# Attention's preparation folded into the attention stage: four token tiles in front, twelve in the loop

## The chip, the cores and the metric

The kernel runs on one core of a Trainium2 chip. A core has a matrix engine (TensorE, PE in the rows; PEld are its weight loads), a vector engine (VectorE, DVE), a scalar engine (ScalarE, ACT), a general engine (GpSimd, POOL) and a queue engine that issues transfers (SyncE, SP). PSUM is the memory that PE writes its results to, SBUF the working memory, DRAM the memory outside. The metric is the device time of one execution in microseconds (us); lower is better.

## What is computed

Four batches of 512 tokens with 512 features pass two layers. The part that matters here is the attention of the second layer:

```python
x = x + _L0_xattn_ref(ctx_512, _layernorm(x), ...)      # graph attention
x = x + _L0_ffn_ref(_layernorm(x), ...)                 # 32 experts, top 4
x = x + _L1_xattn_ref(_layernorm(x), ctx_512, ctx_512)  # this stage
x = x + _L1_ffn_ref(_layernorm(x), ...)                 # 32 experts, top 8

def _L1_xattn_ref(q, k, v):          # q [4, 512, 512], k = v = ctx_512 [4, 512, 128]
    D = 512 // 32; G = 32 // 8       # 16 per head, 4 query heads per key head
    qh = q.reshape(B, S, 8, 4, 16).transpose(0, 2, 3, 1, 4)
    kh = k.reshape(B, S, 8, 16).transpose(0, 2, 1, 3)
    scores = einsum('bkgsd,bktd->bkgst', qh, kh) / sqrt(16)
    out = einsum('bkgst,bktd->bkgsd', softmax(scores), vh)
```

## The kernel before

Five stages run one after the other, each with its own semaphores and a barrier of all engines at its end: `graph_attention`, `open_ffn`, `attention_prepare` (L1576), `attention` (L1758), `capped_ffn`. The change touches the third and the fourth.

**Preparation.** Queries and keys are handed to attention as sums of three bf16 parts (`PARTS`), so that bf16 products of parts give an fp32 result. A unit is one 128x512 tile to be turned: 4 units of keys (one for each batch, four 128x128 pieces of `ctx_sb`) and 16 of tokens. For a token unit DVE computes statistics (L1721 to L1726), ACT the square root (L1683), DVE the scale and shift (L1731, L1732), and ACT or DVE in turn the normalised tile `xn` (L1692, L1739). PE transposes the four pieces into one of four PSUM banks (L1676). ACT rounds to the first part (L1699), DVE takes the difference `left` (L1754), ACT rounds that to the second part (L1703), POOL subtracts again for the third (L1644). SP stores each part to the DRAM tensors `q_parts` and `k_parts`, three transfers for a unit (L1656, L1659). Four places (`PLACES`) of parts are used in turn; a place is written again when its stores have landed (`stored`).

**Attention.** There are 32 groups: 4 batches by 8 key heads, with 4 query heads each. For a group the contraction rows of `kT` and `qT` hold seven products of parts, named by `K_PART` and `Q_PART` (7 x 16 = 112 rows, `PAIR_ROWS`), and 3 rows for the negated row maxima (115, `ROWS_ALL`). In front of the loop SP loads the keys of batch 0 and the queries of groups 1 to 3, ACT the queries of group 0, then the context and, once batch 0's keys have landed, the keys of the other batches (L2038 to L2047). The row maxima of groups 0 and 1 are computed ahead (`LEAD` = 2): per group eight pairs of matmuls (`maximum`, L1938) into two PSUM tiles, each pair reduced by DVE (L2074). POOL splits the maxima into parts (`split_maxima`, L2135 to L2140), PE transposes them (L1968), ACT copies them to `mrows` (L2029), and SP moves them into `qT` by three DMAs (`put_maxima`, L1873) and waits until they have landed.

The loop has one body for each group, with the work of three groups in it. PE issues 16 score matmuls of the group G (L1948), each freed for reuse by ACT's exponential (L2023); the 8 pairs of maxima of G + 2; the weighting of values with the exponentials (`weigh`, L1959), in four steps; the transposes of the maxima of G + 1 and of the output of G - 1 (L1976). Scores, maxima and output take turns in three PSUM banks (`SR` = 3), in an order that `use` writes down at build time (`uses`, `frees`). ACT runs the 16 exponentials, and copies the maxima and the output (L2035). DVE reduces the maxima and divides the output (L2079, L2083), POOL splits maxima, takes the values of the next group (L2148) and adds the old tokens (L2158). SP's body waits until all scores of G are done, loads the queries of G + 4 by seven transfers (L1867), puts the maxima of G + 2, waits for the new tokens (`x_ready`), stores them (L1907) and loads old tokens (L1884):

```python
                def body(G, k, ahead):
                    if not known(G) or G + QR < GROUPS:
                        sp.wait_ge(s_ps, G * SCORES + SCORES)
                        load_q(G + QR, k)
                    if ahead:
                        put_maxima(G + LEAD, (k + LEAD) % QR)
                    sp.wait_ge(x_ready, G + 1)
```

The semaphore waits and the program order on each engine are all that sets the order of the work.

## Time and profile before

| | |
|---|---|
| median of 3 runs | 2141.94 us (2138.0 to 2146.16) |
| the profiled execution | 2139.37 us |
| its span in the trace | 2137.6 us |
| mean granted TensorE clock | 0.909 of full speed |
| busy: PE, DVE, ACT, POOL | 84%, 66%, 50%, 41% |
| preparation, first to next stage's first instruction | 1149.65 to 1211.66 us |
| attention's first instruction to first score matmul | 1211.66 to 1254.88 us |
| attention's loop and end | 1254.88 to 1650.98 us, the next stage's first transfer |

A row of the timeline gives start and duration in us, engine, line of the kernel, operation, output and inputs, a count, and in brackets how long the engine was idle before and what ended that. "SPq" and "ACTq" are transfers issued by SP and ACT; their duration is that of issuing, not of moving the data. In a view of windows PEclk is the granted TensorE clock as a share of full speed, and DMA share the mean busy share of the 16 DMA engines.

### The profile page before, as it was taken

What the parts mean: (1) busy time and instruction counts of PE and PEld (TensorE: products, weight loads), DVE (VectorE), ACT (ScalarE), POOL (GpSimd) and SP (SyncE); (2) the same over time, 40 slices, a digit from 0 to 9 for tenths busy, and PEclk for the clock granted to TensorE, in tenths of its full rate; (3) what the DMA queues carried; (4) which work ended last, traced back from release to release, by engine and by line L of the source; (5) the groups of instructions that cost most, each with busy time, mean ns of one, the idle gap of its engine ahead of it and who ended that gap; (6) DMA issues with size and microseconds to landing.
All of it is one profiled execution on the core that took longest, in us unless ns stands there. A gap on an engine that the chain in (4) does not pass through costs nothing. (4 is left out here: it accounts for less than half of the span.)

```text
span 2137.6 us, 32682 instructions
## 1 busy us (share of the span) xinstructions
PE 1795.9 (84%) x9679; PEld 1025.0 (48%) x9679; DVE 1406.1 (66%) x2807; ACT 1062.3 (50%) x2149; POOL 881.9 (41%) x949
## 2 busy tenths in 40 slices
PE   4689877998548999999993279999997539999997
PEld 2344443444334555555551123333332538888885
DVE  5887877788684666566553478888883765545543
ACT  5588877878332333333332347777776412222222
POOL 5476676668103545555542311111111014444442
PEclk8699988999768999999996579999999759999998
DMA  5111211111455889889655752222221718999993
GB/s 148 55 40 40 83 62 55 40 46 35 147 152 126 177 189 236 224 196 230 122 103 157 158 103 62 57 69 56 62 64 44 267 42 221 230 235 234 230 236 58
DMA packets 202146, 272.01 MB, mean 127 GB/s; under 512 B 83484, under 2 KB 121852, under 8 KB 200956
## 3 DMA queue, kind: packets, MB, share of 16 engines
q1 hardware_dynamic: 156315, 166.52, 25.9%
q0 software_dynamic: 38544, 97.02, 22.5%
q10 hardware_dynamic: 7121, 6.44, 1.6%
q8 instruction: 82, 1.34, 0.3%
q14 instruction: 84, 0.69, 0.1%
HBM read 200.25 MB, written 69.17 MB: 126 GB/s over the span
## 5 line engine op out<-in xcount | busy, mean ns | idle before, releaser
L2074 DVE TENSOR_REDUCE a_negmax<-a_m 128x2 f32<-128x1024 f32 x256 | 304.2, 1221 | 97.2 <-PE a_m L1938 97.2
L291 POOL TENSOR_TENSOR g_near<-g_mask,g_tb 128x512 f32<-128x512 f32 x256 | 322.5, 1282 | 100.0 <-DVE g_emin L545 99.1
L2023 ACT ACTIVATE a_prob<-a_s 128x512 f32<-128x512 f32 x512 | 274.3, 595 | 83.4 <-PE a_s L1948 83.3
L1464 PE MATMUL f_gu_bank<-f_wgu,f_xT 128*128 x768 | 265.5, 489 | 2.9 <-ACT f_xT L1512 2.9
L1258 PEld LDWEIGHTS s_gu_bank<-s_xT,s_wgu 128*128 128x128 f32 x2048 | 240.8, 193 | 31.8 <-issue 27.5
L374 PE MATMUL g_pt<-g_ident,g_p 128*128 128x128 f32 x1024 | 173.5, 299 | 87.1 <-DVE g_pT L554 82.1
L1258 PE MATMUL s_gu_bank<-s_xT,s_wgu 128*128 128x128 f32 x2048 | 241.4, 277 | 1.6 <-ACT s_xT L1288 1.6
L1426 POOL DMA_INDIRECT out<-f_y,f_ids x96 | 151.2, 1575 | 209.5 <-DMA out<-f_y,f_ids 167.6
L475 ACT ACTIVATE g_p<-g_e,g_emin 128x512 f32<-128x512 f32 x256 | 183.4, 716 | 96.0 <-DVE g_emin L545 95.2
L374 PEld LDWEIGHTS g_pt<-g_ident,g_p 128*128 128x128 f32 x1024 | 122.3, 150 | 217.5 <-DVE g_pT L554 142.5
L1464 PEld LDWEIGHTS f_gu_bank<-f_wgu,f_xT 128*128 128x128 f32 x768 | 146.3, 191 | 125.8 <-issue 48.6
L554 DVE COPY g_pT<-g_pt 128x512 f32<-128x512 f32 x256 | 175.3, 685 | 44.5 <-PE g_pt L374 43.1
L545 DVE CUSTOM_DVE_ANT_0 g_e<-g_near,g_h 128x512 f32<-128x512 f32 x256 | 173.0, 676 | 39.9 <-issue 27.0
L1948 PE MATMUL a_s<-a_qT,a_kT 115*128 115x512 bf16 x512 | 179.8, 385 | 8.0 <-DMA a_qT<-a_mrows 6.6
L1938 PE MATMUL a_m<-a_kT,a_qT 112*128 112x512 bf16 x512 | 160.2, 396 | 27.3 <-DMA a_kT<-a_one_rows 25.1
L1234 POOL DMA_INDIRECT out<-s_y,s_ids x64 | 101.7, 1588 | 192.8 <-ACT s_y L1294 167.3
L1481 PE MATMUL f_y_bank<-f_wd,f_actT 96*128 x384 | 180.5, 593 | 0.0
L460 ACT ACTIVATE g_h<-g_tb,g_s 128x512 f32<-128x512 f32 x256 | 172.8, 675 | 0.0
L1542 DVE COPY f_actT<-f_at_bank 96x256 f32<-96x256 f32 x96 | 40.4, 421 | 171.8 <-PE f_at_bank L1473 170.2
L1404 POOL DMA_INDIRECT f_row<-f_x_rows,f_ids x96 | 102.2, 1064 | 106.4 <-issue 103.7
L1319 DVE TENSOR_SCALAR s_den<-s_en 128x256 f32<-128x256 f32 x64 | 20.1, 315 | 184.3 <-ACT s_en L1301 111.9
L404 PE MATMUL g_o<-g_pT,g_feat 128*64 128x512 f32 x512 | 137.8, 640 | 0.9 <-DVE g_res L578 0.9
(291 smaller groups left out, 2767.2 us busy)
## 6 DMA issues: line engine op xcount, KB each, us to landing
s_wgu<-in_L_ffn_w_gate_up SPq DMA_DIRECT2D x32, 1024.0 KB
f_wgu<-in_L_ffn_gate_up_proj SPq DMA_DIRECT2D x32, 768.0 KB
s_wd<-in_L_ffn_w_down SPq DMA_DIRECT2D x32, 512.0 KB
a_qT<-q_parts SPq DMA_DIRECT2D x217, 64.0 KB, 2.4
g_tb<-neighbours SPq DMA_DIRECT2D x8, 1536.0 KB, 8.0
f_wd<-in_L_ffn_down_proj SPq DMA_DIRECT2D x32, 384.0 KB
q_parts<-p_part SPq DMA_DIRECT2D x48, 128.0 KB, 2.3
g_tb<-neighbours SPq DMA_DIRECT2D x8, 512.0 KB, 4.3
```

The lines of the kernel that those rows point to most:

```text
L291: pool.tensor_tensor(near[:, n % LAG, :], mask[slot][:, local % NT, :], t_all[k % SLOTS][:, local // NT, :], ALU.add).then_inc(near_ready, 1)
L374: last = nc.tensor.transpose(pt_bank[n % PT_BANKS][:, c, :], prob[:, n % PROBS, c * P:(c + 1) * P], ident[:, :])
L460: nc.scalar.activation(h_bank[n % H_BANKS][:, :], t_all[k % SLOTS][:, h, :], ACT.Relu, scale=4.0, bias=s_high[k % SLOTS][:, t, h:h + 1]).t ...
L475: nc.scalar.activation(prob[:, n % PROBS, :], eneg[:, n % LAG, :], ACT.Exp, scale=-1.0, bias=emin[:, n % LAG:n % LAG + 1], accum_out=rsum[ ...
L545: V.tensor_tensor_reduce(out=eneg[:, n % LAG, :], in0=near[:, n % LAG, :], in1=h_bank[n % H_BANKS][:, :], scale=-1.0, scalar=3.0e38, op0=A ...
L554: V.tensor_copy(probT[:, n // PAIR % RING, hh, :, t * P:(t + 1) * P], pt_bank[n % PT_BANKS][:, :, :]).then_inc(pt_ready, 1)
L1258: last = nc.tensor.matmul(gu_bank[j % TR][:, f, :], wgu[:, e % RE, c, f * P:(f + 1) * P], xT[j % TR][:, c, :], start=(c == 0), stop=(c == ...
L1464: last = nc.tensor.matmul(gu_bank[j % TR][:, 0:F], xT[j % TR][:, c, :], wgu_flat[:, bass.ds(place_of[j] + c * F, F)], start=(c == 0), stop ...
L1481: last = nc.tensor.matmul(y_bank[j % TR][:, :], actT[j % TR][:, c, :], wd_flat[:, bass.ds(place_of[j] + c * D, D)], start=(c == 0), stop=( ...
L1948: nc.tensor.matmul(bank_of("score", G, n)[:, :], group_keys(G, ROWS_ALL, slice(tt * P, (tt + 1) * P)), qT[k][0:ROWS_ALL, head, :], start=T ...
L2023: nc.scalar.activation(prob[n][:, :], bank_of("score", G, n)[:, :], ACT.Exp).then_inc(p_ready, 1)
L2074: V.tensor_reduce(negmax[k % RING][:, 2 * half:2 * half + 2, head], m_bank[i % RING][:, :, :], X_AXIS, ALU.max, negate=True).then_inc(m_re ...
```

## The change

`attention_prepare` goes. Its work becomes part of `attention`:

- In front of the loop eight units are done: keys of batch 0, the four token tiles of batch 0, then keys of batches 1 to 3. They use the PSUM tiles of the maxima (`m_bank`). The parts of a unit lie in one tile, and one transfer stores all three.
- The other twelve token tiles are done in the loop, one for each of groups 0 to 3 and 8 to 15 (`late_at`): PE transposes it between two score matmuls into a bank of the ring of three, ACT copies it out (`copy_unit`), and POOL makes all three parts and the difference (`all_parts`). Tiles 4 to 7 are normalised by ACT in front of the loop, tiles 8 to 15 by POOL, each in the body of the group ahead. Their statistics are DVE's, in groups 2 to 5, and the square root is ACT's, in the middle of group 6.
- SP loads the keys of batches 1 to 3 in the loop, two transfers in each of four groups; the values of a batch are copied in groups 0 to 2.
- `q_parts` has another layout: the features within a chunk of 128 are ordered by depth, then by head, and the orders of `K_PART` and `Q_PART` are changed, so that the queries of a group come by three transfers in place of seven, of 48, 48 and 16 rows.
- SP stores a unit's parts behind the transfers of its body; the first key units and the loads of `kT` and `qT` are issued in a new order.

The diff, cut ("..." marks what is left out; the removed stage is left out whole, `root`, `first_part`, `second_part`, `statistics`, `variances`, `scales`, `difference`, `third_part` and `copy_values` do what their likes in the removed stage did):

```diff
-K_PART = (0, 0, 0, 1, 1, 2, 1)
-Q_PART = (0, 1, 2, 0, 1, 0, 2)
+K_PART = (0, 0, 0, 1, 1, 1, 2)
+Q_PART = (0, 1, 2, 0, 1, 2, 0)
...
-    TURN_AT, OUT_AT = 9, 7
+    DC = D // P
+    TURN_AT, OUT_AT, UNIT_AT = 9, 7, 4
+    PLACES = 4
+    units = [("keys", 0)] + [("tokens", t) for t in range(NT)] + [("keys", b) for b in range(1, B)]
+    FIRST = len(units)
+    units += [("tokens", t) for t in range(NT, TT)]
+    late_group = list(range(NT)) + list(range(KV, KV + 2 * NT))
+    late_at = {G: i for i, G in enumerate(late_group)}
+    Q_RUNS = ((0, PARTS), (PARTS, PARTS), (2 * PARTS, 1))
+    FINAL_STATS = 6
...
+                if n == UNIT_AT and G in late_at:
+                    use(("unit", late_at[G]), turned_ready, late_at[G] + 1)
...
+        def by_head(row):
+            return row.rearrange("p (c x d) -> p c x d", c=DC, d=HD)
+
+        def by_depth(row):
+            return row.rearrange("p (c d x) -> p c x d", c=DC, d=HD)
...
-                    flat = q_parts.rearrange("j b f s -> j (b f) s")
-                    for r, j in enumerate(Q_PART):
-                        sp.dma_start(qT[k][r * HD:(r + 1) * HD, :, :],
-                                     flat[j, bass.ds(G * GD, GD), :].rearrange("(h d) s -> d h s", d=HD)).then_inc(q_in[k], 16)
+                    b, g = divmod(G, KV)
+                    if g == 0 and b > 0:
+                        for r in range(PLACES):
+                            sp.wait_ge(stored[r], 16 * (2 + b))
+                    heads = q_parts[b, g // 2, :, :, :].rearrange("j (d x) s -> (j d) x s", x=2 * GQ)[:, g % 2 * GQ:(g % 2 + 1) * GQ, :]
+                    for r, count in Q_RUNS:
+                        sp.dma_start(qT[k][r * HD:(r + count) * HD, :, :], heads[0:count * HD, :, :]).then_inc(q_in[k], 16)
...
+                def load_keys(b, r):
+                    if r == 0:
+                        sp.wait_ge(stored[b], 16 * 2 if b else 16)
+                    if r < len(K_PART):
+                        sp.dma_start(kT[r * HD:(r + 1) * HD, b * KV:(b + 1) * KV, :],
+                                     k_parts[b, K_PART[r], :, :].rearrange("(h d) t -> d h t", h=KV)).then_inc(k_in[b], 16)
...
+                def store(u):
+                    what, i = units[u]
+                    for j in range(PARTS):
+                        sp.wait_ge(part_ready[j], u + 1)
+                    if what == "keys":
+                        target = k_parts[i, :, :, :].rearrange("j p (c s) -> p c j s", c=DC)
+                    else:
+                        target = q_parts[i // NT, :, :, :, i % NT * P:(i % NT + 1) * P].rearrange("c j p s -> p c j s")
+                    sp.dma_start(target, part[:, u % PLACES, :, :, :]).then_inc(stored[u % PLACES], 16)
+
+                def load_tokens(first, count, s):
+                    sp.dma_start(tok[:, first:first + count, :],
+                                 tokens[first * P:(first + count) * P, :].rearrange("(t p) d -> p t d", p=P)).then_inc(tok_in[s], 16)
...
+                load_tokens(0, NT // 2, 0)
+                load_tokens(NT, NT, 2)
                 sp.wait_ge(consts, 4)
-                sp.dma_start(kT[PAIR_ROWS:ROWS_ALL, 0:KV, :], bass.AP(one_rows, 0, [[N, PARTS], [0, KV], [1, N]])).then_inc(k_in[0], 16)
+                load_keys(0, len(K_PART))
+                for u in range(3):
+                    store(u)
+                for r in range(len(K_PART)):
+                    load_keys(0, r)
+                for u in range(3, 5):
+                    store(u)
+                for t in range(NT):
+                    sp.wait_ge(stored[(1 + t) % PLACES], 16 * ((1 + t) // PLACES + 1))
+                load_q(0, 0)
                 load_q(1, 1)
-                sp.wait_ge(k_in[0], 16 * (len(K_PART) + 1))
+                for u in range(5, FIRST):
+                    store(u)
...
+                    if G < 2:
+                        load_tokens((2 + G) * NT, NT, 3 + G)
+                    b, step = G // KV + 1, G % KV - 1
+                    if b < B and 0 <= step < 4:
+                        load_keys(b, 2 * step)
+                        load_keys(b, 2 * step + 1)
+                    if G in late_at:
+                        store(FIRST + late_at[G])
...
+                def late_unit(i):
+                    if i < NT:
+                        pe.wait_ge(xn_act, NT // 2 + i + 1)
+                    else:
+                        pe.wait_ge(xn_pool, i - NT + 1)
+                    bank_free("unit", i)
+                    turn(FIRST + i, bank_of("unit", i))
...
+                    if i == 0 and G % KV == 0:
+                        pe.wait_ge(k_in[G // KV], 16 * (len(K_PART) + 1))
                     if i == 0:
-                        pe.wait_ge(q_in[k], 16 * len(Q_PART) * (G // QR + 1))
+                        pe.wait_ge(q_in[k], 16 * len(Q_RUNS) * (G // QR + 1))
...
+                for u in range(FIRST):
+                    first_unit(u)
+                pe.wait_ge(left_ready, FIRST)
                 for G in range(LEAD):
                     for i in range(PAIRS):
                         maximum(G, G, i)
...
+                        if n + 4 == UNIT_AT and G in late_at:
+                            late_unit(late_at[G])
                         if d < NT - 1:
...
+                act.dma_start(ctx_sb[:, 0:NT, :], ctx_dram[0, :, :].rearrange("(t p) f -> p t f", p=P)).then_inc(ctx_in[0], 16)
+                act.dma_start(tok[:, NT // 2:NT, :], tokens[NT // 2 * P:N, :].rearrange("(t p) d -> p t d", p=P)).then_inc(tok_in[1], 16)
+                act.dma_start(ctx_sb[:, NT:TT, :], ctx_dram[1:B, :, :].rearrange("b (t p) f -> p (b t) f", p=P)).then_inc(ctx_in[1], 16)
+                first_part(0)
+                second_part(0)
+                root(0, NT, 0)
+                norm(0)
+                norm(2)
+                first_part(1)
+                for u in range(2, FIRST):
+                    first_part(u)
+                    second_part(u - 1)
+                second_part(FIRST - 1)
+                root(NT, NT, 1)
+                for t in range(NT, 2 * NT):
+                    norm(t)
...
+                        if n + 1 == UNIT_AT and G in late_at:
+                            copy_unit(late_at[G])
+                        if n + 1 == 2 * GQ and G == FINAL_STATS:
+                            root(2 * NT, 2 * NT, 2)
...
+                statistics(range(NT // 2))
+                difference(0)
+                statistics(range(NT // 2, NT))
+                variances(0, NT)
+                scales(0, NT, 0)
+                norm(1)
+                norm(3)
+                for u in range(1, FIRST):
+                    difference(u)
+                copy_values(0)
+                statistics(range(NT, 2 * NT))
+                variances(NT, NT)
                 for G in range(LEAD):
                     for i in range(PAIRS):
                         maximum(G, G, i)
...
+                        if G == 0 and i == 2:
+                            scales(NT, NT, 1)
...
+                    if G + 1 < B:
+                        copy_values(G + 1)
+                    if FINAL_STATS - 4 <= G < FINAL_STATS:
+                        t = 2 * NT + 2 * (G - FINAL_STATS + 4)
+                        statistics(range(t, t + 2))
+                    if G == FINAL_STATS - 1:
+                        variances(2 * NT, 2 * NT)
+                    if G == FINAL_STATS:
+                        scales(2 * NT, 2 * NT, 2)
...
+                def all_parts(i):
+                    u = FIRST + i
+                    source = turned[i % RING][:, :].rearrange("p (c s) -> p c s", c=DC)
+                    pool.wait_ge(turned_ready, i + 1)
+                    pool.wait_ge(stored[u % PLACES], 16 * (u // PLACES))
+                    pool.tensor_copy(part_of(u, 0), source).then_inc(part_ready[0], 1)
+                    pool.wait_ge(part_ready[0], u + 1)
+                    pool.tensor_tensor(left_of(u), source, part_of(u, 0), ALU.subtract).then_inc(left_ready, 1)
+                    pool.wait_ge(left_ready, u + 1)
+                    pool.tensor_copy(part_of(u, 1), left_of(u)).then_inc(part_ready[1], 1)
+                    pool.wait_ge(part_ready[1], u + 1)
+                    pool.tensor_tensor(part_of(u, 2), left_of(u), part_of(u, 1), ALU.subtract).then_inc(part_ready[2], 1)
...
+                def norm(t):
+                    pool.wait_ge(scale_ready, 3)
+                    pool.wait_ge(unit_ps, FIRST + t - 2 * NT + 1)
+                    pool.tensor_scalar(by_depth(xn[:, t % NT, :]), by_head(tok[:, t, :]), rstd[:, t:t + 1], nbias[:, t:t + 1], ALU.mult, ALU.add).then_inc(xn_pool, 1)
+
                 def take_values(G, k):
+                    if G % KV == 0:
+                        pool.wait_ge(val_all_ready, G // KV + 1)
...
+                for u in range(FIRST):
+                    third_part(u)
                 split_maxima(0, 0)
-                pool.wait_ge(val_all_ready, 1)
-                pool.sem_inc(turns, 1)
                 take_values(0, 0)
 
                 def body(G, k, ahead):
                     if not (known(G) and G == GROUPS - 1):
                         split_maxima(G + 1, (k + 1) % QR)
                         take_values(G + 1, (k + 1) % QR)
+                    if G in late_at:
+                        all_parts(late_at[G])
                     if not (known(G) and G == 0):
                         add_tokens(G - 1, (k - 1) % QR)
+                    if G + 1 in late_at and late_at[G + 1] >= NT:
+                        norm(late_at[G + 1] + NT)
...
-    q_parts = nc.dram_tensor("q_parts", (PARTS, B, D, N), BF16).ap()
-    k_parts = nc.dram_tensor("k_parts", (PARTS, B, ctx_512.shape[2], N), BF16).ap()
+    q_parts = nc.dram_tensor("q_parts", (B, D // P, PARTS, P, N), BF16).ap()
+    k_parts = nc.dram_tensor("k_parts", (B, PARTS, P, N), BF16).ap()
...
-    attention_prepare(nc, tokens, ctx_512, q_parts, k_parts)
```

Three places in the order of instructions. PE, body of group 2 of the loop; L1948/L1892 are scores, L1938/L1882 maxima, L1959/L1903 `weigh`, L1976/L1920 the output's transposes. Before:

```order
L1959 MATMUL a_o<-a_prob,a_val 32x512 x4
L1948 MATMUL a_s<-a_qT,a_kT 128x512 x2
L1938 MATMUL a_m<-a_kT,a_qT 128x512 x2
L1948 MATMUL a_s<-a_qT,a_kT 128x512
L1938 MATMUL a_m<-a_kT,a_qT 128x512 x2
L1976 MATMUL a_s<-a_ident,a_oT 128x128 x4
```

and now:

```order
L1903 MATMUL a_o<-a_prob,a_val 32x512 x4
L1851 MATMUL a_s<-a_ident,a_xn 128x128 x4
L1892 MATMUL a_s<-a_qT,a_kT 128x512 x2
L1882 MATMUL a_m<-a_kT,a_qT 128x512 x2
L1892 MATMUL a_s<-a_qT,a_kT 128x512
L1882 MATMUL a_m<-a_kT,a_qT 128x512 x2
L1920 MATMUL a_s<-a_ident,a_oT 128x128 x4
```

The four transposes of a token tile stand between the weighting and the next scores.

ACT, groups 6 and 7; L2023/L1969 are exponentials, L2029/L1975 the copy of maxima, L2035/L1981 the copy of the output. Before:

```order
L2035 ACTIVATE a_oT<-a_o 128x512
L2023 ACTIVATE a_prob<-a_s 128x512 x5
L2029 ACTIVATE a_mrows<-a_s 12x512
L2023 ACTIVATE a_prob<-a_s 128x512 x11
L2035 ACTIVATE a_oT<-a_o 128x512
```

and now:

```order
L1981 ACTIVATE a_oT<-a_o 128x512
L1969 ACTIVATE a_prob<-a_s 128x512 x4
L1985 ACT_TABLE_LOAD
L1985 ACTIVATE a_std<-a_std 128x8
L1969 ACT_TABLE_LOAD
L1969 ACTIVATE a_prob<-a_s 128x512
L1975 ACTIVATE a_mrows<-a_s 12x512
L1969 ACTIVATE a_prob<-a_s 128x512 x11
L1981 ACTIVATE a_oT<-a_o 128x512
```

The square root stands in the middle of the exponentials, with a table load on either side.

SP, from the start of the preparation to the first `put_maxima` (L1873/L1770). Before:

```order
L1648 DMA p_ctx<-in_ctx 128x16x128
L1650 DMA p_tok<-out 128x4x512 x4
L1656 DMA k_parts<-p_part 128x512 x12
L1659 DMA q_parts<-p_part 128x4x128 x48
L1629 UNCONDITIONAL_BRANCH
L1862 UNCONDITIONAL_BRANCH
L1887 DMA a_kT<-k_parts 16x8x512 x7
L1889 DMA a_kT<-a_one_rows 3x8x512
L1867 DMA a_qT<-q_parts 16x4x512 x21
L1884 DMA a_x_old<-out 128x4x64 x2
L1873 DMA a_qT<-a_mrows 1x4x512 x6
```

and now:

```order
L1764 DMA a_tok<-out 128x2x512
L1764 DMA a_tok<-out 128x4x512
L1750 DMA a_kT<-a_one_rows 3x8x512
L1761 DMA k_parts<-a_part 512x3x128
L1761 DMA q_parts<-a_part 128x12x128 x2
L1747 DMA a_kT<-k_parts 16x8x512 x7
L1761 DMA q_parts<-a_part 128x12x128 x2
L1741 DMA a_qT<-q_parts 48x2048 x2
L1741 DMA a_qT<-q_parts 16x2048
L1741 DMA a_qT<-q_parts 48x2048 x2
L1741 DMA a_qT<-q_parts 16x2048
L1761 DMA k_parts<-a_part 512x3x128 x3
```

Of 60 stores in front of the first loads of keys and queries three stand there now, and five in front of the first queries.

## Rows read from the trace of the kernel before

**Rows 1.** Windows view of core 0, one row for each stretch; columns in its first row.

```profile
core 0: us, PE busy (x) PEld busy (x) DVE busy (x) ACT busy (x) POOL busy (x), PEclk, DMA share, GB/s
1149.65:1171.65 22.00, 6.67 (x28) 5.56 (x28) 9.52 (x20) 8.55 (x14) 5.26 (x6) 0.58 0.88 298
1171.65:1211.65 40.00, 13.29 (x52) 9.72 (x52) 25.36 (x53) 21.21 (x39) 19.13 (x16) 0.54 0.67 165
1211.65:1225.65 14.00, 0.00 (x0) 0.00 (x0) 0.00 (x0) 0.02 (x1) 1.53 (x7) 0.50 1.07 127
1225.65:1254.85 29.20, 16.99 (x36) 2.97 (x36) 20.18 (x20) 1.87 (x2) 2.76 (x14) 0.50 1.03 177
1254.85:1645.85 391.00, 387.68 (x2268) 132.54 (x2268) 301.31 (x302) 301.84 (x575) 64.83 (x241) 0.99 0.21 56
```

**Rows 2.** Timeline, start of preparation: start, duration, engine, line, operation.

```profile
1149.71 0.90 SPq L1648 DMA_DIRECT2D p_ctx<-in_ctx  x1
...
1159.05 2.47 DVE L1721 BATCH_NORM_STATS2 p_stats<-p_tok 128x6 f32<-128x512 f32 x4 [28.73 <-DMA p_tok<-out]
...
1163.41 1.28 ACT L1683 ACT_TABLE_LOAD   x1
...
1164.70 0.20 ACT L1683 ACTIVATE p_std<-p_std 128x4 f32<-128x4 f32 x1
```

**Rows 3.** Timeline, start of attention.

```profile
1211.66 3.89 SPq L1887 DMA_DIRECT2D a_kT<-k_parts  x7
...
1225.68 1.86 PE L1938 MATMUL a_m<-a_kT,a_qT 112*128 112x512 bf16 x4 [25.06 <-DMA a_kT<-a_one_rows]
...
1226.73 9.42 DVE L2074 TENSOR_REDUCE a_negmax<-a_m 128x2 f32<-128x1024 f32 x8 [22.41 <-PE a_m L1938]
```

**Rows 4.** Groups by line from 1140 to 1256 us: count, busy us, mean ns, idle before.

```profile
L1644 POOL TENSOR_TENSOR p_part<-p_left,p_part 128x512 bf16<-128x512 f32 x20 | 23.9, 1205 | 32.3 <-ACT p_part L1703 31.9 <-DVE p_left L1754 0.4
...
L1703 ACT ACTIVATE p_part<-p_left 128x512 bf16<-128x512 f32 x20 | 12.5, 625 | 8.1 <-DVE p_left L1754 8.1
...
L1699 ACT ACTIVATE p_part<-p_bank 128x512 bf16<-128x512 f32 x20 | 11.8, 588 | 29.0 <-PE p_bank L1676 23.9 <-DMA q_parts<-p_part 4.9 <-DMA k_parts<-p_part 0.2
```

**Rows 5.** Timeline, end of the start of attention.

```profile
1237.31 7.00 ACTq L2047 DMA_DIRECT2D a_kT<-k_parts  x7
...
1240.16 9.42 DVE L2074 TENSOR_REDUCE a_negmax<-a_m 128x2 f32<-128x1024 f32 x8 [4.00 <-PE a_m L1938]
...
1244.96 19.84 SPq L1873 DMA_DIRECT2D a_qT<-a_mrows  x6
...
1254.88 1.04 PE L1948 MATMUL a_s<-a_qT,a_kT 115*128 115x512 bf16 x2 [6.57 <-DMA a_qT<-a_mrows]
```

**Rows 6.** Timeline of ACT, one group of the loop.

```profile
1399.67 2.12 ACT L2023 ACTIVATE a_prob<-a_s 128x512 f32<-128x512 f32 x4 [0.72 <-PE a_s L1948]
1402.51 2.12 ACT L2023 ACTIVATE a_prob<-a_s 128x512 f32<-128x512 f32 x4 [0.72 <-PE a_s L1948]
1405.05 0.60 ACT L2035 ACTIVATE a_oT<-a_o 128x512 f32<-128x512 f32 x1 [0.43 <-PE a_o L1959]
...
1417.28 0.60 ACT L2035 ACTIVATE a_oT<-a_o 128x512 f32<-128x512 f32 x1 [0.43 <-PE a_o L1959]
```

**Rows 7.** Timeline of SP's DMA issues in the same group.

```profile
1409.71 1.82 SPq L1873 DMA_DIRECT2D a_qT<-a_mrows  x3
1412.72 0.40 SPq L1907 DMA_DIRECT2D out<-a_x_new  x1
...
1413.72 3.34 SPq L1867 DMA_DIRECT2D a_qT<-q_parts  x7
```

**Rows 8.** Timeline of DVE and POOL in the same group.

```profile
1412.55 2.36 DVE L2074 TENSOR_REDUCE a_negmax<-a_m 128x2 f32<-128x1024 f32 x2 [0.48 <-PE a_m L1938]
...
1415.10 0.20 POOL L2135 CAST a_mbf<-a_negmax 128x16 bf16<-128x16 f32 x1 [6.22 <-DVE a_negmax L2074]
```

**Rows 9.** DMA view, 1400 to 1500 us: median us from issue to landing.

```profile
a_qT<-q_parts SPq DMA_DIRECT2D x58, 64.0 KB, 2.3
```

289 lines of the change are left out of this document (114 added, 175 removed).

## The prediction

> **What bounds the kernel now.** I first cut the span into stretches with the windows view [rows 1]. The first three, 76.0 us, are the preparation, its barrier and the loads of keys and queries; in the third no engine but POOL works. The fourth, 29.2 us, is the row maxima of the first two groups. The fifth, 391 us, is the loop, where PE is busy at a granted clock of 0.99 (2.4 GHz) and POOL for 65 us. So the change can win in the first four (105 us, before the first score) and lose in the fifth. The page's chain of waits is of no use here, since it reaches back only into the last stage.
>
> Next I read who waits in those stretches. The preparation starts on transfers: DVE's statistics come 9.4 us after its start (1159.05), behind 2 MB in one queue [rows 2]. From there a unit costs ACT 588 + 625 ns and POOL 1205 ns, 20 times [rows 4]; 40 us for its second part is more than 1.2 us a unit. Attention's first matmul then waits 25 us, the last 14 of them for keys and queries (1211.66 to 1225.68) [rows 3]. The loop is a cycle between PE and ACT: four exponentials, 0.72 us of waiting for the next score, 2.84 us in all; a group is 12.23 us (1405.05 to 1417.28) [rows 6]. DVE waits 0.48 us in each round of two reductions, POOL 6.2 us at a stretch [rows 8].
>
> **The work in front of the loop.** I measure from 1149.65 to the first reduction of maxima, 1226.73 [rows 3]: 77.1 us. In the new order (all are estimates from the rows named):
> - Loads. Two queues issue smaller first pieces: 0.25 MB of context, then tokens in pairs. With 2 MB landed in 9.4 us [rows 2], I put the first statistics at 6.5 us and the second pair at 8.
> - Scales. Before, statistics start at 1159.05 and the root runs at the end of the table load, 1164.69, 5.6 us later [rows 2]. The table load now lies beside the second pair; I take root at 10.3, first normalised tile at 11.6, its transposes at 12.9.
> - Units 1 to 4 at 1.25 us each (ACT, POOL [rows 4]): the third part of unit 1 is ready at 16.3, of unit 2 at 17.5, of unit 4 at 20.
> - SP stands in the way once: behind the store of unit 2 come seven loads of keys, 3.9 us of issue [rows 3], so unit 3 is stored at 22. The keys are 0.9 MB; the third stretch moved 127 GB/s, with the transfer engines fully busy [rows 1], so they take 7 us, and the stores of units 3 and 4 queue behind them: landed at 28.5.
> - Queries of group 0: 1.6 us of issue for three transfers (0.48 each before [rows 7]) and 2.3 us to land [rows 9]: 32.5. A matmul pair and its wait add 1.05 (1225.68 to 1226.73 [rows 3]): **33.5 us**. DVE has finished the last difference, the values and four statistics at about 32.5, so it doesn't come later.
>
> Gain 77.1 - 33.5 = **43.6 us**. Bounds: 29 if the keys come at twice that rate and units never wait for a place; 40 if each store lands only behind all of the 3 MB of loads.
>
> **From the first reduction to the first score** it took 28.2 us (1226.73 to 1254.88): two times 9.4 us of reductions, 4.0 us of splitting and transposing between them, and in the end a wait of 6.6 for the maxima's rows [rows 3, 5]. ACT couldn't copy the maxima before 1244.3, since it issued 21 key loads until then (ACTq, 7.0 us the last seven), and the rows issued at 1244.96 took 9.9 us among them to be used [rows 5]. The key loads are now SP's, in the loop. What is left is 9.4 + 4 + 9.4 = 22.8: gain **5.3 us** (3 to 6).
>
> The barrier goes with the stage; its 2 to 5 us are within the 77.1. Instructions of the preparation don't vanish, twelve units of 20 move.
>
> **Twelve units in the loop.** Each adds four transposes to PE and a copy to ACT, in front of the same score. The output has the same pair, and so have the maxima: 12.23 - 4 x 2.84 = 0.87 us for both [rows 6], so 0.43 us each, since the 0.60 us copy runs beside transposes. At this place ACT already has the output's copy behind its 0.43 us wait [rows 6], so a second copy there can't hide in that wait; PE's four transposes run beside the first. I take 0.55. The ceiling is both in a row, 0.60 + 0.57 = 1.17. 12 x 0.55 = **6.6 us** (5.2 to 14).
>
> POOL gets four operations of at most 1.2 us and, for the last eight, a normalisation: 6.2 us against 6.2 of idle time at a stretch and 2.5 more ahead of it [rows 4, 8]. The new tokens come up to 3.5 us later, while SP is still waiting for its maxima's rows until 1412.72 [rows 7]. Cost nothing; if that cover is gone, the store of x slips, which nobody waits for in under a group.
>
> **Square root in group 6.** ACT does load, root, load: 1.28 + 0.20 + 1.28 = 2.76 us [rows 2], of which the round's wait of 0.72 [rows 6] hides one: **2.0 us** (2.0 to 2.8). In the row the root follows the load at once (1163.41 + 1.28, then 1164.70), nothing more is paid. The Trainium skill (ScalarE: Activation LUTs, What ACT_TABLE_LOAD costs) counts a drain of about 1.38 us for each switch as well; by that page it would be an estimated 4.8, and the rest of this text stands without it.
>
> **DVE's extra work** in groups 0 to 5: statistics of a pair 1.23 us (2.47 / 2 [rows 2]) in groups 2 to 5, a copy of values of about 0.4 in groups 0 to 2, and the variances of eight tiles, about 1 us, in group 5. It comes between two groups, where 0.48 us of wait [rows 8] and the slack of the second PSUM tile (I put it at 0.7: PE is let go by the reduction before the last) take it up: nothing for 0.4, 0.1 for 1.23, 0.5 for 1.6 (group 2), 1.1 for 2.2 (group 5): **1.8 us**. Floor 0, ceiling all of it, 7.5.
>
> **SP in the loop.** Seven query transfers of 3.34 us of issue [rows 7] become three, 1.6; two key loads (1.0) and a store (0.5) come in. Issue hardly changes, and is off the path. What is queued behind is `put_maxima`, which is the next rival's matter.
>
> **Sum.** 43.6 + 5.3 - 6.6 - 2.0 - 1.8 = 38.5 us. Against the profiled execution, 2139.37 - 38.5 = 2100.9; the median of the runs was 2.6 above that execution, so **2103 us**.
>
> **Rivals.**
> - *The terms of the loop are near their ceilings* and the front at 36: gain 41.1 + 3, less 14 + 2.8 + 7.5: 20 us, **2122 us**. For it: the path between PE and ACT has no slack in any round. Against: two like pairs cost 0.43 each. Chance 0.14.
> - *The front is bound by transfers.* The keys and queries of attention's start took 14 us with no compute beside them [rows 1, 3]; now token loads, stores in 256-byte pieces and key loads share that time. With the first reduction at 50 us, 16.5 later: **2119 us**. Against: the second stretch moved 165 GB/s of such stores at a transfer share of 0.67 [rows 1], so they are not slow by nature. Chance 0.12.
> - *POOL sets the pace of twelve groups.* The Trainium skill (GPSIMD Engine Reference, Key points) says that POOL shares its SBUF interfaces with DVE. In this trace POOL's subtraction with DVE beside it is 1205 ns [rows 4]. If all five new operations took twice that, POOL's group would be 12 + 2.1 + 1.3 = 15.4 us against 12.8: 12 x 2.6 = 31 us back, **2134 us**, no measurable change. Chance 0.04.
> - *Slower: the maxima's rows land late.* `put_maxima` is issued at 1409.71 and its rows are needed by the next group's first score, some 4.6 us later (that score stands 0.4 us ahead of the exponentials of 1402.51, and 12.23 later is 1414.3 [rows 6]); landed they were by 1412.72 [rows 7]. At the start, beside the key loads, it took 9.9 us [rows 5]. Keys, stores or tokens are now in flight in 17 groups; if the rows took 9.9 us in each, 17 x 5.3 = 90 us: **2193 us**. It decides from 6.9 us of landing, where 17 x 2.3 eats the gain. Against: these transfers are issued behind the previous rows, most of a group ahead. Chance 0.04.
> - *Faster:* front at 29 (4.5 more), units at 0.43 (1.4), DVE hidden (1.8): **2095 us**. Chance 0.14.
>
> **How the numbers follow.** The forecast, 2103 with 2098 to 2110 of its own, has 0.52. The range takes in the faster case and the first two rivals: 2092 to 2122, with about 0.1 outside. 0.5%, 10.7 us, is about what a measurement of this kernel can tell from no change: the forecast, the faster case and the first two rivals are faster by more (0.92); POOL's case and a part of the late rows' are the same (0.05); slower 0.03.
>
> **What would show it.** Right: no second barrier; the first reduction 33 us after the first transfer, the first score 23 later; groups 0 to 3 and 8 to 15 about 0.55 longer than 12.23, group 6 by 2, the others the same; after group 15 exactly 12.23. Wrong in the front: PE's first maxima end a wait for `a_qT` later than 40 us. Wrong in the loop: "DMA a_qT<-a_mrows" as what ends PE's waits, or POOL without idle time. The forecast fails outright if the late rows do that in more than a few groups.

## The result, and the profile after

The changed kernel takes **2111.9 us** (median of 4 runs, 2110.66 to 2114.33) where the kernel before, on the same chip, takes 2142.14 (4 runs, 2138.0 to 2146.16): ratio 0.9856, 95% interval 0.9843 to 0.9869, so 30 us or 1.4% faster. In two later sets of runs, on two chips, it was 23 us (1.1%) and 32 us (1.3%) faster than the kernel before beside it. The forecast was 2103 with 2092 to 2122. The profiled execution took 2110.66 us, with a span of 2108.9.

The time between two marks of the trace tells more than the whole, because the stages ahead of this one vary: in the profiles of the changed kernel and its variants the first transfer of the stage starts anywhere from 1149.2 to 1160.0 us. Here, before and after have it at the same time (1149.71 [rows 2] and 1149.57). All positions below are counted from it.

| part of the stage | before | after | difference | forecast |
|---|---|---|---|---|
| first transfer (before: 1149.65, as the forecast counts it) to first reduction of maxima | 77.1 | 36.8 | -40.3 | -43.6 |
| first reduction to first score | 28.2 | 21.65 | -6.5 | -5.3 |
| first score to the last copy of maxima's rows | 373.7 | 394.7 | +21.0 | +10.4 |
| from there to the end of the program | 509.0 | 506.2 | -2.8 | 0 |

The last line can't be told from no effect: in the twelve profiles of the experiments the same code takes 505.1 to 509.6 us there.

Windows view of the changed kernel, in the columns of [rows 1]: front, the maxima of the first two groups, the loop.

```profile
1149.60:1186.30 36.70, 7.44 (x35) 6.25 (x36) 13.57 (x31) 13.02 (x21) 10.88 (x15) 0.55 0.86 193
1186.30:1208.00 21.70, 15.79 (x36) 2.67 (x34) 17.63 (x17) 6.35 (x6) 1.40 (x7) 0.50 0.49 106
1208.00:1620.80 412.80, 398.63 (x2317) 137.44 (x2315) 310.30 (x328) 311.65 (x590) 118.14 (x304) 0.98 0.32 76
```

Against [rows 1], four stretches of 105 us have become two of 58, and POOL is busy for 118 us of the loop instead of 65. PE, busy for all but 3 of 391 us of the loop before, is now idle for 14 of 413.

The front, in the timeline of the changed kernel (start, duration, engine, line, operation, and in brackets the idle time before it and who ended it):

```profile
1153.67 1.29 DVE L2057 BATCH_NORM_STATS2 a_stats<-a_tok 128x6 f32<-128x512 f32 x2 [23.43 <-DMA a_tok<-out]
...
1168.41 3.57 SPq L1747 DMA_DIRECT2D a_kT<-k_parts  x7
...
1171.33 0.60 ACT L1997 ACTIVATE a_part<-a_m 128x512 bf16<-128x512 f32 x1 [0.49 <-DMA q_parts<-a_part]
...
1172.09 2.83 SPq L1761 DMA_DIRECT2D q_parts<-a_part  x2
...
1179.55 0.60 ACT L1997 ACTIVATE a_part<-a_m 128x512 bf16<-128x512 f32 x1 [7.10 <-DMA q_parts<-a_part]
...
1180.97 2.66 SPq L1741 DMA_DIRECT2D a_qT<-q_parts  x6
...
1185.29 1.87 PE L1882 MATMUL a_m<-a_kT,a_qT 112*128 112x512 bf16 x4 [17.60 <-DMA a_qT<-q_parts]
...
1207.99 1.06 PE L1892 MATMUL a_s<-a_qT,a_kT 115*128 115x512 bf16 x2
```

The stores of units 3 and 4 are issued behind the seven key loads at 22.5, and the first of them lands at 30.0, when ACT gets its place back after 7.1 us of waiting. The query loads follow at 31.4, and PE has the queries at 35.7. PE waits 17.6 us, and of what it waits for the queries land last by the profile.

The surprise is in the loop. In the view of PE's waits in it the first line is new (who waits for whom, us in total, times, longest); in the second the longest, 1.7 us, is new too, and is PE's wait at the square root:

```profile
PE a_m L1882 <- DMA a_kT<-a_one_rows: 8.2, 3, 3.0
PE a_s L1892 <- ACT a_prob L1969: 3.0, 6, 1.7
```

The turn of the loop can be read from ACT's copies of the maxima's rows, one in a group. Around the first of these waits:

```profile
1278.58 0.57 ACT L1975 ACTIVATE a_mrows<-a_s 12x512 bf16<-12x512 f32 x1
...
1292.76 1.28 ACT L1985 ACT_TABLE_LOAD   x1
1294.06 0.21 ACT L1985 ACTIVATE a_std<-a_std 128x8 f32<-128x8 f32 x1
1294.28 1.28 ACT L1969 ACT_TABLE_LOAD   x1
1295.58 0.60 ACT L1969 ACTIVATE a_prob<-a_s 128x512 f32<-128x512 f32 x1
1296.07 0.57 ACT L1975 ACTIVATE a_mrows<-a_s 12x512 bf16<-12x512 f32 x1
```

That is 17.49 us for the turn of group 6. All 31 turns, in order of their groups from 0, worked out in this way:

```
before:  18.04, then 29 of 12.22 or 12.23, 11.64
after:   16.43, 12.71, 12.71, 12.74, 12.40, 12.41, 17.49, 12.00,
         12.71, 12.70, 12.71, 12.71, 12.70, 12.71, 18.28, 12.70,
         12.23, 12.23, 12.22, 12.23, 12.23, 12.22, 16.78, then 12.22 or 12.23, 11.65
```

Groups 6, 14 and 22 are the ones in which PE starts the maxima of the next batch (`G + LEAD` is 8, 16, 24), and so first needs its keys. PE and SP in group 6 (turn's start 1278.58):

```profile
1283.77 0.61 PE L1892 MATMUL a_s<-a_qT,a_kT 115*128 115x512 bf16 x2
1287.36 0.61 PE L1882 MATMUL a_m<-a_kT,a_qT 112*128 112x512 bf16 x2 [2.98 <-DMA a_kT<-a_one_rows]
```

```profile
1279.18 1.84 SPq L1770 DMA_DIRECT2D a_qT<-a_mrows  x3
1282.23 0.40 SPq L1814 DMA_DIRECT2D out<-a_x_new  x1
1282.66 0.51 SPq L1781 DMA_DIRECT2D a_x_old<-out  x1
1283.22 0.53 SPq L1747 DMA_DIRECT2D a_kT<-k_parts  x1
1283.78 0.82 SPq L1750 DMA_DIRECT2D a_kT<-a_one_rows  x1
```

SP's body for group 4 issues the last two transfers of the keys. But it waits for that group's new tokens, which come while PE is in group 5, and so it issues them at 1283.8, when PE wants them at 1284.4. They are 3.0 us late.

### The profile page after: what moved, and what is told of

Same layout as the page of the kernel before. It is cut to its first block and busy times, and to the rows that moved or that the text cites. A ratio compares the mean times of both kernels' runs of the same rounds, so it can differ in the third digit from the quotient of the medians.

```text
span 2108.9 us, 32488 instructions
## 1 busy us (share of the span) xinstructions
PE 1788.2 (85%) x9679; PEld 1016.9 (48%) x9679; DVE 1388.2 (66%) x2786; ACT 1059.5 (50%) x2135; POOL 918.2 (44%) x991
## 3 DMA queue, kind: packets, MB, share of 16 engines
q0 software_dynamic: 38544, 97.02, 22.5%
## 5 line engine op out<-in xcount | busy, mean ns | idle before, releaser
L1969 ACT ACTIVATE a_prob<-a_s 128x512 f32<-128x512 f32 x512 | 274.8, 595 | 90.6 <-PE a_s L1892 89.3
L1258 PEld LDWEIGHTS s_gu_bank<-s_xT,s_wgu 128*128 128x128 f32 x2048 | 240.3, 193 | 31.8 <-issue 27.5
L1882 PE MATMUL a_m<-a_kT,a_qT 112*128 112x512 bf16 x512 | 161.6, 399 | 28.4 <-DMA a_qT<-q_parts 17.6
L1892 PE MATMUL a_s<-a_qT,a_kT 115*128 115x512 bf16 x512 | 180.9, 386 | 3.2 <-ACT a_prob L1969 3.0
```

The lines of the kernel that those rows point to most:

```text
L1258: last = nc.tensor.matmul(gu_bank[j % TR][:, f, :], wgu[:, e % RE, c, f * P:(f + 1) * P], xT[j % TR][:, c, :], start=(c == 0), stop=(c == ...
L1892: nc.tensor.matmul(bank_of("score", G, n)[:, :], group_keys(G, ROWS_ALL, slice(tt * P, (tt + 1) * P)), qT[k][0:ROWS_ALL, head, :], start=T ...
L1969: nc.scalar.activation(prob[n][:, :], bank_of("score", G, n)[:, :], ACT.Exp).then_inc(p_ready, 1)
```

## The experiments

**Theory.** The front and the units cost about what was forecast. The 10 us missing in the loop are the keys: at each change of batch PE waits for them, and what comes on top of the wait is a lower clock behind it and the table load. **Rivals.** The long turns come from the stored queries, the statistics or the table load; SP's queue is too full; or the front, not the loop, has the difference.

### Keys one group earlier

```diff
-                    b, step = G // KV + 1, G % KV - 1
+                    b, step = G // KV + 1, G % KV
```

> The key loads of the next batch are spread over groups G % 8 = 0 to 3 of the loop, one group earlier than in the changed kernel; nothing else differs. In the changed kernel's trace three turns of ScalarE's loop are long, those of groups 6, 14 and 22 (17.49, 18.28 and 16.78 us, against 12.7, 12.7 and 12.23 around them), and in them TensorE's first maxima of the next batch wait for the last rows of the keys. Theory A (the last keys land too late for the first maxima of the next batch): the last of them now lands 12 us before it is wanted, the turns of groups 14 and 22 fall back to 12.7 and 12.2, that of group 6 to between 12.7 and 15.5 (what is left is the table load of the last square root), and the whole falls by 9 to 14 us to 2098 to 2103. Rival B (the long turns come from something else at the change of a batch, the waits for the stored queries or the statistics): the three turns stay, and the time is within 2 us of 2112. Rival C (SyncE's queue is too full in groups 0 to 3, where it also loads tokens): turns 14 and 22 are cured, but maxima rows in groups 1 to 4 go behind the key loads, and the gain is under 5 us.

**Measured:** 2102.12 us (4 runs), 0.9799 of the kernel before (0.9774 to 0.9823). The waits for the keys are gone from PE's list, and turns 14 and 22 are 12.71 and 12.23. Turn 6:

```profile
1280.53 0.57 ACT L1975 ACTIVATE a_mrows<-a_s 12x512 bf16<-12x512 f32 x1
...
1295.94 0.57 ACT L1975 ACTIVATE a_mrows<-a_s 12x512 bf16<-12x512 f32 x1
```

15.41 us. The sum of turns 1 to 30 is 374.9 against 387.1: the late keys cost **12.2 us** in the first profile. Two more profiles of the unaltered kernel have 385.3 and 385.6, so there they cost 10.4 and 10.7. Theory A holds, with turn 6 at the upper end of what it gave. Rivals B and C fall: the long turns are gone, and turns 1 to 5 are what they were. Turn 6 keeps 3.2 us over 12.23, more than root and table loads (2.8) last; the run without the root, below, takes it apart.

**The same again**, beside the changed kernel on another chip:

> The kernel with the keys one group earlier, again: 9 to 12 us below the changed kernel of the same call; turn 6 at 15.4, turns 14 and 22 at 12.7 and 12.2.

**Measured:** 2104.34 (5 runs), turns 6, 14 and 22 at 15.41, 12.71, 12.23 as told.

> The changed kernel on the same chip as the others of this call: turns 6, 14 and 22 long by 3 to 7 us each, 3.0 us of TensorE's wait for the keys in each, whatever the chip; ratio to the kernel before 0.985 to 0.990.

**Measured:** 2113.44 (6 runs), ratio 0.9871 (0.9843 to 0.9898). Turns 6, 14 and 22 are 17.59, 15.48 and 18.02, 5.2, 2.8 and 5.8 longer than the turns before them; PE's waits in them are 3.09, 2.60 and 2.61, so two of the three are below the 3.0 that was told. 9.1 us lie between the two, 10.2 between their traces (440.9 and 451.1 us from the first transfer to the last copy of maxima).

### Keys two microseconds earlier

The key loads stay in their groups and move ahead of SP's wait for the new tokens (the same four lines go from their old place behind it, not shown):

```diff
+                    b, step = G // KV + 1, G % KV - 1
+                    if b < B and 0 <= step < 4:
+                        load_keys(b, 2 * step)
+                        load_keys(b, 2 * step + 1)
                     sp.wait_ge(x_ready, G + 1)
                     sp.dma_start(group_tokens(G), x_new[k % RING][:, :, :]).then_inc(x_stored[k % RING], 16)
...
```

> The key loads of the next batch stay in the groups where the changed kernel has them, but within a group SyncE issues them ahead of its wait for the new tokens instead of behind their store and the load of the old ones: for the last two of a batch (row of ones among them) that is 1283.2 us to about 1281.1 in the first trace, 2.1 us earlier. Theory A (TensorE waits for the landing of the last keys, and its clock can fall behind the wait): the wait of 3.0 us shrinks by what the issue is earlier, to 0.6 to 1.2 us in each of three turns, the clock stays at 1.00, turns 14 and 22 are 12.8 to 13.6 us long, turn 6 has its 15.4, and the whole is 8 to 11 us below the changed kernel. Rival B (the length of the turn is set by the number of transfers in flight, not by when the keys are issued): the wait stays at 3 us. Rival C (the new tokens' store, now later, holds something else up): another wait appears, on the loads of old tokens.

**Measured:** 2105.22 (5 runs), 0.9823 (0.9799 to 0.9848): 8.2 us below the changed kernel on that chip. PE's first wait for the keys:

```profile
1292.78 0.61 PE L1882 MATMUL a_m<-a_kT,a_qT 112*128 112x512 bf16 x2 [1.15 <-DMA a_kT<-a_one_rows]
```

The wait went from 2.98 to 1.15 and turns 14 and 22 to 14.01 and 13.57, each about 1.3 longer than its neighbours (A said 12.8 to 13.6: the first is 0.4 above). The wait didn't stay at 3 us, so B falls, and no new wait for old tokens appears, so C does. Counted from the turn's start the last transfer of the keys is issued at 4.0 us instead of 5.2, and 3.0 us lie between its issue and PE's start instead of 3.6: 1.2 us are the earlier issue, 0.6 a shorter landing. In turns 14 and 22 a wait of 1.1 us costs 1.3. In turn 6 the wait of 1.15 costs 0.26 only (15.67 against 15.41): there PE would otherwise wait for DVE, as shown below. The granted clock is 1.00 behind all three.

### The changed kernel again: the clock

> The changed kernel again, unaltered, beside the others of this call. Theory A: 2110 to 2113 us as before, first maxima 35.5 to 36 us after the stage's first transfer; each of the long turns of groups 6, 14 and 22 holds a 3 us wait of TensorE for the keys and is 15.4 to 15.6 us long where the granted clock stays at 1.00 behind the wait, and 18.0 to 18.5 where it falls to 0.50 (the turn of group 6 has the table load besides). Rival: the turns have fixed lengths of 17.5, 18.3 and 16.8 us as in the first profile, and the clock has no part in them.

**Measured:** 2124.48 (6 runs, 2115.09 to 2128.89), beside 2147.74 of the kernel before (11 runs, 2138.05 to 2158.57): ratio 0.9888 (0.9856 to 0.992). The whole missed: 2110 to 2113 was expected. The trace puts it outside this stage: its first transfer is at 1159.59 instead of 1149.57, the part behind the last copy of maxima is 2.8 us longer, and between the two it took 452.0 us against 453.1. Why the other stages took longer is open.

Turns 6, 14 and 22 are 18.97, 15.48 and 16.30, so the same turn has no fixed length; turn 14 was 18.28 in the first profile. What differs is the clock. Windows of PE around the same wait (us, busy, granted clock, DMA share, GB/s), first in the first profile of the changed kernel (turn of 18.28), then in its third (15.48):

```profile
1389.50:1392.62 3.12, 0.61 (x7) 0.89 0.87 191
1392.62:1398.00 5.38, 5.38 (x18) 0.50 0.37 105
1398.00:1402.00 4.00, 4.00 (x24) 0.91 0.01 2
```

```profile
1390.29:1393.49 3.20, 0.60 (x7) 1.00 0.85 192
1393.49:1399.00 5.51, 5.51 (x34) 1.00 0.35 98
1399.00:1403.00 4.00, 4.00 (x29) 1.00 0.02 7
```

The waits are alike, 2.51 and 2.60 us. Behind the first, PE is at 1.2 GHz for over 5 us and does 18 matmuls where it did 34 at 2.4 GHz behind the second; the turn is 2.8 us longer. In the six profiles that have the keys as the changed kernel has them (18 waits of 2.5 to 3.9 us) the clock stood at 0.50 behind 11 of them. It did so in all six turns 22, in four turns 6 and in one turn 14. What decides in which, these runs don't show: waits of 2.5 and 2.6 us are on both sides. How long the clock stays down sets the length. Over its neighbours, turn 14 is 2.7 to 2.9 us longer in the five profiles in which the clock stays at 1.00 (waits of 2.53 to 2.76 us); turn 22 is 4.1 to 4.6 longer where the clock is down for some 3 us behind the wait, and 5.8 to 6.0 where it is for some 6; the one turn 14 with the clock down for 6 us is 5.6 longer. Theory A holds in its kind and misses a size: it had 18.0 to 18.5 wherever the clock falls, and turn 22 is 16.30 with a fall. The rival (fixed lengths) falls.

### No square root in the loop

```diff
-                    nc.scalar.activation(std[:, first:first + count], std[:, first:first + count], ACT.Sqrt).then_inc(std_done, 1)
+                    nc.scalar.activation(std[:, first:first + count], std[:, first:first + count], ACT.Copy if g == 2 else ACT.Sqrt).then_inc(std_done, 1)
```

> The square root in the loop (group 3's step, for the tokens of batches 2 and 3) is replaced by a copy of the same tile, so the square root of the variances of batches 2 and 3 is left out; ScalarE then loads no other table in the loop. Theory A (in the long turn the table loads lie beside the wait for the keys or add to it): the turn with the table load gets shorter by 0.7 to 2.8 us if it is paid, by nothing if the wait for the keys hides it; the whole is 2109 to 2112. Rival B (the table loads and the root make the long turn of group 6 by themselves): that turn falls from 17.5 to 12.7 us, 4.8 less, and the whole to 2107. Turns 14 and 22 stay by all theories.

**Measured:** 2112.78 (4 runs): no gain. Turn 6 got longer, 18.54, since the clock fell to 0.50 behind its wait for the keys (3.11 us), where in the first profile it had stayed. This run could not tell the theories apart. With the keys one group earlier as well, it could:

> Keys one group earlier, as before, and the square root of the variances of batches 2 and 3 replaced by a copy, so that root is left out and no other table is loaded in the loop. Theory A (once no wait for keys covers it, the table load is paid in full: in the run with the keys earlier the turn of group 6 was 15.41 us against 12.23, and the next 12.00): turns 6 and 7 are 12.23 each, and the whole is 2.9 us less than with the keys earlier alone, 2099 us. Rival (the table load is hidden behind TensorE's bound): within 0.5 us of 2102, turn 6 stays long for another reason.

**Measured:** 2101.27 (6 runs, 2097.91 to 2106.66; on a chip on which the kernel before took 2147.74). Turn 6 in the timeline of ACT, and DVE and PE in it:

```profile
1288.79 0.57 ACT L1975 ACTIVATE a_mrows<-a_s 12x512 bf16<-12x512 f32 x1
...
1302.09 0.57 ACT L1975 ACTIVATE a_mrows<-a_s 12x512 bf16<-12x512 f32 x1
```

```profile
1294.50 1.28 DVE L2057 BATCH_NORM_STATS2 a_stats<-a_tok 128x6 f32<-128x512 f32 x2
1295.81 0.65 DVE L2062 BATCH_NORM_AGGREGATE a_mv<-a_stats 128x2 f32<-128x6 f32 x8
1296.49 0.18 DVE L2064 TENSOR_SCALAR a_std<-a_mv 128x8 f32<-128x8 f32 x1
1296.58 3.48 DVE L2096 TENSOR_REDUCE a_negmax<-a_m 128x2 f32<-128x1024 f32 x3
```

```profile
1297.85 0.60 PE L1882 MATMUL a_m<-a_kT,a_qT 112*128 112x512 bf16 x2 [0.42 <-DVE a_negmax L2096]
...
1298.98 0.61 PE L1882 MATMUL a_m<-a_kT,a_qT 112*128 112x512 bf16 x2 [0.31 <-DVE a_negmax L2096]
```

Turns 6 and 7 are 13.30 and 12.23, against 15.41 and 12.00 with the root: the root with its two table loads costs 27.41 - 25.53 = **1.9 us** (a copy of 0.20 us stands in the root's place, so the normalised tokens of batches 2 and 3 lack the root). By the traces from first transfer to last copy it is the same (440.7 less 438.8). Theory A had 2.9 and missed the other 1.07, which I put down to DVE: two statistics and the variances of eight tiles delay the next reduction, and PE waits for it twice, 0.73 us in all. No run leaves them out, so this cause is read from the rows and not shown by taking it away. The run with the keys earlier has the same two waits (0.42 and 0.31); the changed kernel has none, since there the wait for the keys covers them. PE's wait at the table loads is not covered by it. It is 1.71 us in both kernels, here in the changed one:

```profile
1296.23 0.39 PE L1892 MATMUL a_s<-a_qT,a_kT 115*128 115x512 bf16 x1 [1.71 <-ACT a_prob L1969]
```

### The unit at another place in its group

Keys one group earlier, and:

```diff
-    TURN_AT, OUT_AT, UNIT_AT = 9, 7, 4
+    TURN_AT, OUT_AT, UNIT_AT = 9, 7, 12
```

> Keys one group earlier, and the late units' transposes and ScalarE's copy of them stand behind score 11 instead of score 3 of their group. Theory A (a late unit costs what TensorE's four transposes take, wherever they stand): 0.48 us in each of 12 groups as before, the whole within 1 us of 2102. Rival B (the cost is a bank of the scores given to the unit, and ScalarE's copy that stands ahead of an exponential): the cost changes with the place, to between 0 and 1.2 us a group, 2096 to 2111 in all. Rival C (POOL gets the unit too late behind the split of the maxima, and the store of the parts lands later): no change in the turns, since the queries are wanted 4 groups later.

**Measured:** 2107.31 (6 runs, 2104.13 to 2123.39), and from first transfer to last copy 444.2 us, 3.5 more than with the keys earlier alone. The usual turn with a unit is 12.71 at both places, so a unit costs **0.48 us** at both, as A says. The whole is not within 1 us of 2102, as A also said: turn 3 is 15.45, turn 4 12.88 and turn 14 13.31, none of which any of the theories told. Two waits in turn 3 of this kernel:

```profile
1252.96 0.60 PE L1892 MATMUL a_s<-a_qT,a_kT 115*128 115x512 bf16 x2 [1.84 <-DMA a_qT<-a_mrows]
...
1254.22 0.60 PE L1882 MATMUL a_m<-a_kT,a_qT 112*128 112x512 bf16 x2 [0.66 <-DMA a_qT<-q_parts]
```

This is the slower rival of the forecast, the maxima's rows that land late, once. The rows give the chain. POOL's program has the unit ahead of the new tokens, and POOL now waits 6.18 us for ACT's copy of the unit (0.72 in the same group with the unit at its old place). So SP gets the new tokens later and stores them 37.0 us behind the first copy of maxima's rows instead of 32.2, and issues the maxima's rows of the next group, which stand behind that in its queue, at 45.2 instead of 41.9. Here the cover is gone of which the forecast said that without it only the store of x slips: what slips is the whole queue behind it. In turn 14 a score waits 0.53 us for a reduction by DVE, which is about what that turn has too much.

### Query transfers by seven

```diff
-                    for r, count in Q_RUNS:
-                        sp.dma_start(qT[k][r * HD:(r + count) * HD, :, :], heads[0:count * HD, :, :]).then_inc(q_in[k], 16)
+                    for r, j in enumerate(Q_PART):
+                        sp.dma_start(qT[k][r * HD:(r + 1) * HD, :, :], heads[j * HD:(j + 1) * HD, :, :]).then_inc(q_in[k], 16)
...
-                        pe.wait_ge(q_in[k], 16 * len(Q_RUNS) * (G // QR + 1))
+                        pe.wait_ge(q_in[k], 16 * len(Q_PART) * (G // QR + 1))
```

> The queries of a group go by seven transfers of 16 rows each, as in the kernel before, instead of three of 16, 64 and 32 rows; nothing else differs. Theory A (three transfers save issue time of SyncE only): six transfers for units 0 and 1 in front become fourteen at 0.6 us each, so the first maxima start 2 to 3 us later, and in the loop, where SyncE has 8 us to spare in a group of 12.2, nothing changes: 2114 to 2115. Rival B (four more issues in each loop group push the maxima rows and the last keys): each of the long turns 6, 14, 22 grows by another 2 us and the whole is 2120 or more. Rival C (seven transfers spread better over the DMA engines than three): front unchanged or shorter, 2110 to 2112.

(The three transfers of the changed kernel are of 48, 48 and 16 rows, not of 16, 64 and 32.)

**Measured:** 2115.51 (4 runs, 2110.43 to 2116.24), which can't be told from the changed kernel. The first maxima start at 36.6 after the first transfer; in the three profiles of the changed kernel they do at 35.6 to 35.9, so A's 2 to 3 us are under 1. Turns 14 and 22 are 15.41 and 16.52, in the span of the others. B falls by them. Turn 6 is 20.02, its wait for the keys 3.9 instead of 3.0, and turn 4 is 12.81 instead of 12.40, with a wait of 0.51 us for the maxima's rows: in these two the longer queue shows. So three transfers for seven bring about 1 us in front, 0.4 in turn 4 and about 1 in turn 6 (20.02 against 18.97 and 19.02, the two others in which the clock was down for as long).

### The front: stores first

```diff
-                for u in range(3):
+                for u in range(5):
                     store(u)
                 for r in range(len(K_PART)):
                     load_keys(0, r)
-                for u in range(3, 5):
-                    store(u)
```

> In front SyncE stores units 0 to 4 and loads the seven parts of the first keys behind them, instead of between the stores of units 2 and 3; nothing else differs. Theory A (in front the stores of units 3 and 4 stand behind the key loads, and ScalarE's wait for a free place, 7.1 us, is the path to the first queries): the wait shrinks to 3 us or less and the first reduction of maxima starts about 4 us earlier, at 33 us after the first transfer instead of 36.8; the whole is 2107 to 2109. Rival B (the transfers themselves are the bound, and the keys just land later): the first reduction is within 1 us of 36.8, the first maxima then wait for the keys instead of the queries, and the whole is within 1 us of 2112.

**Measured:** 2112.05 (4 runs, 2110.41 to 2119.89). SP's issues, and the first maxima, in this kernel (first transfer at 1157.58):

```profile
1174.83 5.69 SPq L1761 DMA_DIRECT2D q_parts<-a_part  x4
1180.56 3.58 SPq L1747 DMA_DIRECT2D a_kT<-k_parts  x7
1184.32 2.64 SPq L1741 DMA_DIRECT2D a_qT<-q_parts  x6
```

```profile
1193.01 1.87 PE L1880 MATMUL a_m<-a_kT,a_qT 112*128 112x512 bf16 x4 [16.68 <-DMA a_qT<-q_parts]
```

```profile
1184.50:1187.50 3.00, 0.00 (x0) 0.50 1.15 124
1187.50:1190.50 3.00, 0.00 (x0) 0.50 1.12 141
```

ACT's 7.1 us of waiting became 0.2, and the query loads went out at 26.7 instead of 31.4. They landed at 35.4 all the same, 8.7 us after their issue instead of 4.3. In the windows between, the DMA share is over 1 at 124 and 141 GB/s. The changed kernel has the same rate while its key loads are under way, and more than twice that behind them, when the stores of units 3 and 4 are:

```profile
1172.50:1177.00 4.50, 0.00 (x0) 0.50 1.15 122
1178.00:1179.50 1.50, 0.00 (x0) 0.50 1.27 287
```

So it is the key loads that fill the transfer engines for long, not the stores. Rival B holds in its first part (the first maxima didn't come earlier); it named the keys as what they wait for, and the profile names the queries, which stand behind them. A falls: in neither kernel was ACT's wait of 7.1 us the path to the first queries.

### The front: only the keys that are wanted

Keys one group earlier, stores first, and then (not shown: the added arguments of `load_keys`, and PE's wait for `k_rest` ahead of group 2's maxima):

```diff
                 for r in range(len(K_PART)):
-                    load_keys(0, r)
+                    load_keys(0, r, 0, LEAD)
...
                 load_q(0, 0)
                 load_q(1, 1)
+                for r in range(len(K_PART)):
+                    load_keys(0, r, LEAD, KV, k_rest)
```

> Keys one group earlier; and in front SyncE stores units 0 to 4 first, then loads of the first batch's keys only those of groups 0 and 1 (seven transfers of 32 KB instead of 128), then the queries of groups 0 and 1, and behind them the keys of groups 2 to 7. Theory A (with the stores first the front did not get shorter, since the transfers of the keys, 896 KB at some 120 GB/s, stood ahead of the queries in the DMA queues): the queries now land within 4.5 us of their issue instead of 9, the first maxima start at 31 to 32 us after the stage's first transfer instead of 35.7, and the whole is 3.5 to 5 us below the kernel with the keys earlier, 2097 to 2099. Rival B (the seven issues on SyncE's queue or the stores of the queries are the path): first maxima at 35 or later, 2101 to 2103. Rival C (group 2's maxima then wait for their keys): the front gains 4 but the wait moves into the loop's first groups, 2100 to 2102.

**Measured:** 2097.83 (6 runs), 0.9771 of the kernel before (0.9741 to 0.9802). The first transfer of this profile is at 1149.20:

```profile
1172.58 3.52 SPq L1749 DMA_DIRECT2D a_kT<-k_parts  x7
1176.27 2.64 SPq L1742 DMA_DIRECT2D a_qT<-q_parts  x6
1178.95 3.25 SPq L1749 DMA_DIRECT2D a_kT<-k_parts  x7
```

```profile
1181.04 1.87 PE L1886 MATMUL a_m<-a_kT,a_qT 112*128 112x512 bf16 x4 [13.62 <-DMA a_qT<-q_parts]
```

Queries land 4.8 us after their issue at 27.1, and the first maxima start at 31.8 instead of 36.05: A, within its numbers but for the landing (4.5 at most). Seven more issues, behind the queries, cost nothing; three quarters of the key bytes taken from ahead of the queries give 4 us, in a kernel that has the stores first. The split without that order was not run.

> The kernel with the keys one group earlier and with the split keys in front, again, beside the one without the split and the changed kernel on the same chip. By the traces (first maxima at 31.8 us after the stage's first transfer against 36.05): 3.5 to 4.5 us below the kernel with the keys earlier alone, and 15 to 16 below the changed one. Rival: the 4 us come from the chip on which it ran; within 2 us of the one without the split.

**Measured:** **2095.77 us** (5 runs, 2093.38 to 2098.8), 0.9772 of the kernel before (0.975 to 0.9795), 8.6 us below the one without the split on the same chip and 17.7 below the changed kernel. The traces give 4.4 us (436.5 against 440.9) to the split; the rest of the 8.6, which is above the 3.5 to 4.5 told, is outside of this stage, or chance of the runs. This is the best version: 2.3% below the kernel before, where the change alone has 1.3% on the same chip.

## Why the prediction was right, and what it missed

The direction and the range held, and the largest term by far, the front, came out at nine tenths of what was forecast. But a term of 12 us was missing, in the loop, and the others were each a little off. The forecast's own narrow band, 2098 to 2110, did not hold. The range did by some luck: it had been drawn for two rivals, neither of which is what happened, and 2.8 us of the gain between the two profiled executions (28.7) lie behind the last copy of maxima, where the change is not seen to do anything.

- **Front: 43.6 forecast, 40.3 measured.** The steps hold one by one at first: statistics at 4.1 instead of 6.5, the root's result at 10.8 instead of 10.3, normalised tile at 11.4 (11.6), transposes at 12.8 (12.9), stores of units 3 and 4 behind the keys at 22.5 (22). The step that was off is "landed at 28.5": they landed at 30.0 and by 31.4. The store of unit 2, 384 KB, had itself landed only at 21.8 (the end of ACT's wait at 1171.33), when the keys had been in the same queue for 2.9 us; the sum began their 7 us at their issue, and gave the stores of units 3 and 4 no time of their own, while 768 KB at the 287 GB/s of the window above take 2.7. Unit 4's third part was ready at 22.6 instead of 20, because ACT has its second part behind unit 5's first, which waited 2.2 us for a place; the key loads covered this. From there the queries took 4.3 us (3.9 forecast). The rival *bound by transfers* was right about the mechanism, as the two runs on the front show, and wrong by 13 us about its size.
- **First reduction to first score: 5.3 forecast, 6.5 measured.** 28.2 - 21.65. No mistake of kind.
- **Twelve units: 0.55 forecast, 0.48 measured** in each group that has one. It lies between the 0.43 of the like pairs in [rows 6] and the forecast, a little nearer to the 0.43. The eleven units behind turn 0 make 5.3 us.
- **POOL: nothing, as forecast.** From the groups by line of the loop after:

```profile
L2198 POOL TENSOR_TENSOR a_left<-a_turned,a_part 128x512 f32<-128x512 f32 x12 | 13.9, 1158 | 1.0
...
L2196 POOL CAST a_part<-a_turned 128x512 bf16<-128x512 f32 x12 | 7.4, 613 | 10.2 <-ACT a_turned L2007 10.2
```

  The subtraction takes 1158 ns, where [rows 4] had 1205, and what DVE does beside it in this loop is mostly a reduction out of PSUM. The rival of a POOL twice as slow falls. That is not to say that DVE never slows POOL: beside a copy by DVE from SBUF to SBUF the same operation took 1.30 us three times in the run with the unit later, and beside DVE's scaling of a token tile 1.43 us once in the kernel before (at 1198.98). The Trainium skill (GPSIMD Engine Reference, Key points) has POOL share its interfaces to SBUF with DVE, with contention for DVE instructions in a 2-port mode or with two SBUF inputs. The rows fit that: 1.15 to 1.16 us beside reductions out of PSUM, 0.14 to 0.27 more beside DVE's copy and scaling within SBUF; in which mode DVE ran no row says.
- **Square root: 2.0 forecast, 1.9 measured**, once nothing else stood beside it. The load, the root and the next load follow each other within 0.02 us (1292.76, 1294.06, 1294.28). The drain of 1.38 us a switch that the Trainium skill (ScalarE: Activation LUTs, What ACT_TABLE_LOAD costs) adds would have made the estimate of 4.8; the measurement decides for 1.9.
- **DVE's extra work: 1.8 forecast, 1.4 read from the turns**: 0.17 and 0.18 in turns 4 and 5, and 1.07 in turn 6 for the variances (1.1 forecast). Group 2's 0.5 is not there (turn 3 has 0.03).
- **Keys in the loop: nothing forecast, 12.2 measured** (10.4 and 10.7 in the other two profiles of the kernel). This is the step that failed: "Two key loads (1.0) and a store (0.5) come in. Issue hardly changes, and is off the path. What is queued behind is `put_maxima`". It asked what stands behind the new loads in SP's queue, and not when the last of them is due and what stands ahead of them: a wait for new tokens that come a group later. The order of issues and PE's `maximum` for group `G + LEAD` told both before any run: last keys in the body of group 4, done in group 5's time, due at the start of group 6. Of the 12.2 us, 2.1 are in turns 6 and 7 (29.49 against 27.41), 5.6 in turn 14 and 4.6 in turn 22. The three waits are 8.2. In turn 6 the clock stays up, and the wait of 2.98 costs 2.1, less than itself, since it covers PE's waits for DVE. In turn 14 the lower clock adds 2.8 to what the same turn costs with the clock up. In turn 22 no profile has the clock up, so its part there is argued.
- *What would show it* said "groups 0 to 3 and 8 to 15 about 0.55 longer, group 6 by 2, the others the same". Groups 14 and 22 contradict it.

Sum of the loop as measured: 5.3 (units) + 1.4 (DVE) + 1.9 (root) + 12.2 (keys) = 20.8, of 21.0. All four are differences of the same turns, so that they add up is no test of its own; the keys and the root are shown by taking them away, the units and DVE are read from the turns.

## What to carry to other kernels

For every transfer that a change moves into a loop, work out two times: when the queue's engine really comes to issue it, with the waits that stand ahead of it, and when its first reader wants it; a body's number is not a time, since engines run groups apart. Where TensorE is the bound, a late operand can cost more than the wait: 2.5 to 3 us of idling cost up to 6 us here, while 1.1 us cost 1.3. Where another wait stands right behind, it costs less: 2.1 for 3.0 in turn 6, and 0.26 for 1.15. And when the DMA engines are full, shortening what stands ahead of the wanted bytes gains (4 us by loading a quarter of the keys first), where only reordering issues gained nothing here.

## What the runs showed of the hardware that I had not expected

- TensorE's clock at 0.50 for some 3 to 6 us behind 11 of 18 idle spells of 2.5 to 3.9 us in the midst of a loop at 1.00, and behind none of the three of 1.1 to 1.2 us.
- Key loads, each a row of 1 KB for a head and depth, run at 122 to 141 GB/s with the DMA engines' share above 1, as in the third stretch of [rows 1] (127). The units' stores, in pieces of 256 bytes, ran at 287 GB/s in the same queue (1178.00 to 1179.50 in the changed kernel), so here the shorter pieces went faster. Whether that is the direction, the order of the addresses or something else, no run shows.
- The stages ahead of this one, not touched here, took up to 11 us more in some profiles than in others (first transfer at 1149.2 to 1160.0); only positions counted from a mark inside the stage made differences of 2 to 4 us readable.
